# A 16-head cross-attention's last unit turned ahead of an awaited transfer, its second batch in a bank of its own, and each layer's last expert rounded two units sooner

## The reference

```python
# per layer in (L0, L2, L3): context 2 x 2048 x 128, mask 2 x 2048
q = (layernorm(x) @ Wq)            # 16 heads of 128
k, v = ctx @ Wk, ctx @ Wv          # 8 heads of 128, each shared by 2 query heads
p = softmax(mask(q @ k.T / sqrt(128)))
x = x + (p @ v) @ Wo
...
# the last block, L3_ffn: a mixture of 8 experts whose weights are first rounded
# to 8-bit floats, with one power-of-two scale for each block of 32
w13q = mxfp8_qdq(w13);  w2q = mxfp8_qdq(w2)
```

## Time and profile before

| | us |
|---|---|
| median of 3 runs | 1428.22 |
| lowest and highest run | 1422.49, 1431.65 |
| the profiled execution | 1422.41 |
| its span, first to last instruction | 1420.7 |
| TensorE matmul / VectorE / ScalarE / GpSimd busy | 87% / 77% / 65% / 21% |

### The profile page before, as it was taken

The page is one execution under the profiler, slowest core; times in us unless marked ns, Lnnn a source line. Parts: engine busy times, 40 slices in busy tenths (PEclk is TensorE's granted clock), DMA queues, the critical chain, the costliest instruction groups (busy, mean ns, idle before and its releaser), DMA issues. The chain is left out here.

```text
span 1420.7 us, 25856 instructions
## 1 busy us (share of the span) xinstructions
PE 1231.3 (87%) x10032; PEld 848.7 (60%) x10036; DVE 1100.1 (77%) x2026; ACT 919.6 (65%) x1285; POOL 296.0 (21%) x231
## 2 busy tenths in 40 slices
PE   4999999648887998875989999987898899999887
PEld 1677777434334555554756767664586567767654
DVE  5787786396888999927588898857598888889563
ACT  3877777454666777833167777756595767677664
POOL 0000000100251111000005264350263062552400
PEclk9999999979999999987999999999899999999999
DMA  6899989102006999996069999860573799889700
GB/s 249 151 174 187 191 162 159 60 0 97 1 1 118 191 195 187 200 191 144 20 123 182 195 184 184 154 157 17 170 205 118 131 166 177 169 171 169 142 11 8
DMA packets 548298, 195.77 MB, mean 138 GB/s; under 512 B 534880, under 2 KB 535264, under 8 KB 546912
## 3 DMA queue, kind: packets, MB, share of 16 engines
q1 hardware_dynamic: 548192, 194.35, 68.4%
HBM read 59.83 MB, written 0.26 MB: 42 GB/s over the span
## 5 line engine op out<-in xcount | busy, mean ns | idle before, releaser
L687 DVE SCALAR_TENSOR_TENSOR arena<-L_xattn_sm,L_xattn_rr,arena 128x1024 f16<-128x1024 f32 x192 | 278.8, 1493 | 12.1 <-ACT arena L578 12.1
L441 PE MATMUL ps<-ctxT,L_xattn_qk 128*128 128x512 f16 x1152 | 266.3, 381 | 1.7 <-DVE L_xattn_qk L654 1.4
L563 ACT ACTIVATE L_xattn_sm<-L_xattn_sm,L_xattn_mx 128x2048 f32<-128x2048 f32 x96 | 192.3, 2003 | 81.2 <-DVE L_xattn_mx L669 80.2
L578 ACT ACTIVATE arena<-L_xattn_sm,L_xattn_rr 128x1024 f16<-128x1024 f32 x192 | 210.0, 1141 | 5.2
L453 PE MATMUL ps<-arena,ctx 128*128 128x128 f16 x2976 | 187.4, 223 | 16.9 <-DMA arena<-arena 16.7
L453 PEld LDWEIGHTS ps<-arena,ctx 128*128 128x128 f16 x2976 | 175.5, 100 | 32.9 <-DMA arena<-arena 21.6
L441 PEld LDWEIGHTS ps<-ctxT,L_xattn_qk 128*128 128x128 f16 x1152 | 111.5, 99 | 128.1 <-issue 3.7
L669 DVE CUSTOM_DVE_ANT_0 L_xattn_sm<-ps,L_xattn_bias 128x1024 f32<-128x1024 f32 x96 | 117.2, 1221 | 69.9 <-issue 69.6
L669 DVE CUSTOM_DVE_ANT_0 L_xattn_sm<-ps,L_xattn_bias,L_xattn_mx 128x1024 f32<-128x1024 f32 x96 | 123.2, 1284 | 0.8 <-DVE L_xattn_mx L669 0.5
L463 PEld LDWEIGHTS ps<-arena,ctx 128*128 128x128 f16 x1488 | 90.8, 98 | 17.1 <-DMA arena<-arena 0.2
L179 PE MATMUL ps<-ctxT,identh 128*128 128x512 f16 x346 | 91.6, 400 | 7.7 <-PEq L353 3.0
(11 more groups left out here) (539 smaller groups left out, 2109.0 us busy)
## 6 DMA issues: line engine op xcount, KB each, us to landing
L_ffn_ring<-in_L_ffn_experts SPq DMA_DIRECT2D x34, 384.0 KB, 3.6
arena<-in_L_xattn_w SPq DMA_DIRECT2D x36, 320.0 KB, 3.9
arena<-in_L_ffn_experts SPq DMA_DIRECT2D x8, 768.0 KB, 7.8
arena<-in_L_xattn_w SPq DMA_DIRECT2D x6, 640.0 KB, 14.0
arena<-arena SPq DMA_TRANSPOSE x193, 4.5
arena<-in_L_ffn_codes SPq DMA_DIRECT2D x1, 3072.0 KB, 10.9
arena<-in_L_ffn_scales SPq DMA_DIRECT2D x8, 384.0 KB, 22.7
arena<-in_L_attn_w SPq DMA_DIRECT2D x1, 2163.0 KB, 8.7
```

The source lines that it names most:

```text
L441: last = nc.tensor.matmul(ps[:, at, :], qk[:, h // 2, qp, h % 2, b * P:(b + 1) * P], k.ctxT[:, cp, b, at * 512:(at + 1) * 512], start=(a = ...
L563: nc.scalar.activation(sm[:, u % 2, :], sm[:, u % 2, :], ACT.Exp, bias=mx[:, u % 2, 1:2], scale=-1.0, accum_out=rs[:, u % 2:u % 2 + 1]).th ...
L578: nc.scalar.mul(pp[:, u % 2, 0, at], sm[:, u % 2, at], rr[:, u % 2:u % 2 + 1]).then_inc(s.p_high, 1)
L687: nc.vector.scalar_tensor_tensor(pp[:, u % 2, 1, at], sm[:, u % 2, at], rr[:, u % 2:u % 2 + 1], pp[:, u % 2, 0, at], ALU.mult, ALU.subtrac ...
```

## The change

- On TensorE in the last iteration, `turn_last(0)` moves ahead of mix_high(30) and `turn_last(1)` ahead of mix_low(30). In the last body mix_last(0) comes ahead of tail_out(head 14).
- Unit 31 is multiplied into bank 6 (`PREP`) in place of the second half of `O[1]`, so that batch 0 of head 15 can be copied out while batch 1 is still being made. Copy, Wv, copy and Wo of head 15 run once for each batch at half width (`mixed_last`, `values_last`, `values_copy_last`, `out_last`), batch 0's among the matmuls of unit 31.
- ScalarE's copies of the turned high part move ahead of `values_copy` of head 14.
- The bodies in which experts' exponents are made go from 0, 8, 16, 24 to 0, 8, 16, 22, and those of the rounds from 3, 11, 19, 27 to 3, 11, 19, 25. This concerns L2 and L3 alone.

```diff
+    EXPONENTS_AT, ROUNDS_AT = (0, 8, 16, 22), (3, 11, 19, 25)
...
@@ mix_last
-                                last = nc.tensor.matmul(O[1][:, P:2 * P], k.ctx[:, cp, KT + kt, :], pt[:, 1, part, kt, :],
+                                last = nc.tensor.matmul(PREP[:, P:2 * P], k.ctx[:, cp, KT + kt, :], pt[:, 1, part, kt, :],
...
+                def values_last(b):
+                    pe.wait_ge(s.oT_ready, XH + b)
+                    at = slice(b * P, (b + 1) * P)
+                    nc.tensor.matmul(TAIL[1 - b][:, at], wv[1], oT[:, at], start=True, stop=True).then_inc(s.oh_psum, 1)
+
+                def out_last(b):
+                    pe.wait_ge(s.oh_ready, XH + b)
+                    nc.tensor.matmul(OUT[:, b * D:(b + 1) * D], oh[:, b * P:(b + 1) * P], wo[1][:, 1, :], start=False,
+                                     stop=True, skip_group_check=True).then_inc(s.out_done, 1)
@@ TensorE's body
                         if final and u == UNITS - 1:
+                            mix_last(0)
                             tail_out(*mixed)
                             break
+                        if final and u == UNITS - 2:
+                            turn_last(0)
                         mix_high(i, u)
...
                         if final and u == UNITS - 2:
-                            turn_last(0)
+                            turn_last(1)
                         mix_low(i, u)
...
                 iterations(pe, body)
-                turn_last(1)
-                mix_last(0)
+                values_last(0)
                 mix_last(1)
-                tail_values(LASTI, BODY - 1, False)
-                tail_out(LASTI, BODY - 1)
+                out_last(0)
+                values_last(1)
+                out_last(1)
@@ ScalarE
+                def mixed_last(b):
+                    at = slice(b * P, (b + 1) * P)
+                    act.wait_ge(s.mixed_lo, XH * B - 1 + b)
+                    nc.scalar.mul(oT[:, at], (O[1], PREP)[b][:, at], 1.0 / XPUP).then_inc(s.oT_ready, 1)
+
+                def values_copy_last(b):
+                    at = slice(b * P, (b + 1) * P)
+                    act.wait_ge(s.oh_psum, XH + b)
+                    act.wait_ge(s.out_done, XH - 1)
+                    nc.scalar.copy(oh[:, at], TAIL[1 - b][:, at]).then_inc(s.oh_ready, 1)
...
+                        if final and u == UNITS - 2:
+                            last_copy(0, 0)
+                            last_copy(0, 1)
                         if head:
                             values_copy(*head, first and u == 2)
...
                 iterations(act, body)
-                last_copy(0, 0)
-                last_copy(0, 1)
                 last_copy(1, 1)
-                mixed_copy(LASTI, BODY - 1)
-                values_copy(LASTI, BODY - 1, False)
+                mixed_last(0)
+                values_copy_last(0)
+                mixed_last(1)
+                values_copy_last(1)
@@ VectorE
-                        if experts is not None and u == 0:
-                            expert_exponents(k, dve, weigh, experts + i)
-                        if experts is not None and u == 3:
-                            expert_rounds(k, dve, weigh, experts + i)
+                        if experts is not None and UNITS * i + u in EXPONENTS_AT:
+                            expert_exponents(k, dve, weigh, experts + EXPONENTS_AT.index(UNITS * i + u))
+                        if experts is not None and UNITS * i + u in ROUNDS_AT:
+                            expert_rounds(k, dve, weigh, experts + ROUNDS_AT.index(UNITS * i + u))
...
-                dve.wait_ge(s.out_done, XH)
+                dve.wait_ge(s.out_done, XH + 1)
```

More of the change, by code:

```diff
@@ L588, in values_copy, with last_copy @@
                     nc.scalar.copy(oh[:], TAIL[h % 2]).then_inc(s.oh_ready, 1)
+                def last_copy(part, half):
+                    act.wait_ge(s.last_psum, 2 * part + half + 1)
+                    act.wait_ge((s.mixed_hi, s.mixed_lo)[part], XH * B - 2)
+                    nc.scalar.copy(pt[:, 1, part, half * KT // 2:(half + 1) * KT // 2, :], TURNED[2 * part + half])\
+                        .then_inc((s.last_hi, s.last_lo1)[part], 1)
+                def mixed_last(b):
[7 more added lines that the diff above has]
+                    nc.scalar.copy(oh[:, at], TAIL[1 - b][:, at]).then_inc(s.oh_ready, 1)
                 def body(i, first, final):
```

## The result

The changed kernel takes 1437.41 us, the median of twelve runs (1432.78 to 1440.93); the kernel before, measured beside it, 1429.30 (twelve runs, 1421.04 to 1431.65). The ratio is 1.0065, with an interval of 1.0048 to 1.0081: 9.3 us slower on 1428, with 6.9 and 11.6 as its ends. That is more than the 5.9 forecast and above the band of +4 to +7.5 that was given 50%; the time lies inside the range of 1426 to 1440.

The account below looks back on a forecast made before the run. VectorE was taken to set when unit 31 is ready in L3, with L2 its twin. L0 -1.5, L2 +3.55, L3 +3.55 and clock +0.3 gave +5.9, or 1434.0 us; 8-in-10 range 1426 to 1440.

Parts of the forecast that it names:

- L0: At L0's end, the reorder alone shortens mix_high(30) to the last addition from 11.53 to 10.0 us: -1.5 us.
- The contention: In L2 and L3, GpSimd's earlier pass lengthens p_low(29) and p_low(30), so invert(31) starts 3.5 us later per layer.
- about one addition: On VectorE in L2 and L3, each half of p_low(29) and p_low(30) is delayed by one GpSimd addition beyond its own 1.24 us.
- The exponents' move: In L2 and L3, making the last expert's exponents after unit 24's p_low costs 0, bounds 0 and +0.5 us.
- The reorder on top: In L2 and L3, turn_last(0) makes TensorE wait for unit 31's high part; mix_high(30) starts at 1323.95, x 10.0 us later.
- The clock: TensorE's idle time before turn_last(0) in L2 and L3 lowers its clock, mostly within the wait: +0.3 us in all.
- half clock in both tails: Rival: TensorE runs at half clock in L2's and L3's tails, +3.4 in place of 0.3, +9.0 us in all; chance 10%.
- GpSimd's hold: At the block's end in L2 and L3, GpSimd's drain no longer holds the block, saving 0.2 us per layer.

Follow-up runs that it names:

- the kernel with the busy matmuls: The changed kernel with 11 unused matmuls on TensorE ahead of turn_last(0) in L2 and L3: 1432.68 us, ratio 1.0036 to the kernel before.

## Why the prediction was right, and where its size was off

**L0: right.** Forecast -1.5, 10.0 from mix_high(30) to the addition; the trace has 10.00. The turn lies inside the wait for the transfer, as forecast, though mix_high(30) starts 0.26 us later behind invert(31) than it did (3.65 for 3.39). That distance goes from 3.2 to 3.6 over the traces, and is 3.6 in the one with the expert alone moved, so the turn need not be the cause. The gain of the whole layer's block was 1.3.

**The contention: right in kind, place and size.** The forecast was made from the rounds' end. Measured from there (1305.58 in L3): p_low(28) at +2.6 taking 3.13 (forecast +2.8, 3.10), the additions at +8.5 (+8.4), p_low(29) at +9.8 taking 4.33 (+8.7, 5.5), p_low(30) at +16.9 taking 4.16 (+17.0, 4.15). Invert(31) comes 28.44 us after scores(28) in L3, 3.3 more than before; forecast 3.5. In L2 it is 29.98, 4.9 more. The experiment without the pass shows the cause, that with the expert alone moved the size (+3.3 in each). Part of the agreement is luck: scores(30), which the forecast left at 12.01 us behind scores(28), came at 13.1 and 13.8, and p_low(29) met less of the pass for it.

The turns that p_low and the additions take are again as the Trainium skill has them (SBUF — State Buffer, section Who interferes with whom): two SBUF inputs on VectorE and a reading instruction of GpSimd exclude each other. The runs agree, 5.57 us with the additions and 2.48 without them. They agree on GpSimd's side too: in the changed kernel's L3 the addition that starts while a half of p_low is running takes 2.79 us, and one that starts while none is takes 1.82. With the latter figure the prediction's "about one addition" for each half, 1.55 us on top of its own 1.24, is about right; the mean of 2.28 us that the earlier trace rows gives contains GpSimd's own waits.

**The exponents' move: mis-sized.** I took 0, with bounds 0 and +0.5. It is 1.3 to 1.4 by itself. The step that failed is the list of what follows the moved instruction: I counted VectorE's 1.9 us and TensorE's wait for a later high part, but not that SP has a load of weights to issue ahead of this unit's transfer, that the two come closer together (1.18 us apart in the changed kernel's L3, for 2.80), and that the transfer then takes 6.8 us to land in place of 4.3. Together with the rounds' move it isn't added in full: in L3 it bought back about as much contention (4.33 in place of 5.57), in L2 hardly any (5.44). So invert(31) came 0.2 us sooner than forecast in L3 and 1.4 later in L2. That this is the exponents' move is argued, from scores(30) coming late; measured against the rounds' move alone it is worth -1.3 and +0.3.

**The reorder on top: right in kind.** Forecast: invert(31) to mix_high(30) 3.2 us, then 10.0, released by ScalarE after an idle time of some 3 us. The idle time was 3.00 and 2.81, released by L592. At full clock the distances were 3.21 and 9.99 (the kernel with the busy matmuls). What the forecast did not see is how much better the other order is in a late tail: 11.5 in place of 13.2, 1.7 us per layer.

**The clock: the term that was too small.** I added 0.3 in all, bounds 0 and 3.4, on the argument that the dip would fall mostly into the wait. It fell behind it. Invert(31) to the last addition took 15.34 and 14.83 in place of 13.2: 3.8 us, over the upper bound, which had allowed 1.7 for a tail. L2's cost 2.1, of which some 1.7 lie in mix_high(30) and 0.4 ahead of it, in the turn. Its rival "half clock in both tails", given 10%, is what happened; it named +9.0. That this is so close to the measured 9.3 is luck in part, since its other terms are the forecast's. The row that should have weighed more is the earlier trace rows's first: 2.2 us of idle time, and 0.57 of the clock over the next 4 us, in one of two places. The idle time foreseen was longer than that, in both layers. The Trainium skill (TensorE: Matmul & The Clock Gate, section The HAM clock gate) says that idleness brings the array back to half its clock; the two windows at 0.50 and 0.65 agree, and the busy matmuls, with 1.00, show that it is this idle time.

**GpSimd's hold: right.** Its drain is over 14 us before the block's end in L3, and the hold, forecast at 0.2 for each layer and in fact 0.3 and 0.2, is gone.

**The sum.** Forecast -1.5 + 3.55 + 3.55 + 0.3 = 5.9. In the same terms the traces have -1.5 (L0), 4.9 + 0.3 in L2 and 3.3 + 0.2 in L3 for invert(31) and the turn ahead at full clock, 3.8 for the clock and -0.5 for the hold: +10.5, or +10.6 with the hundredths. The measurement has 9.3, between 6.9 and 11.6. Of the 4.7 us between the sums 3.5 are the clock and 1.2 is invert(31), 1.4 later than forecast in L2 and 0.2 sooner in L3.

**What stays open.** Why the granted clock differs from one trace to the next in the last block, whose code doesn't change, and why it fell in L2's tail and not in L3's behind idle times of 1.5 to 1.9 us. The reorder alone gains 2.3 to 3.4 by the ratios, where its tails show 1.0 at best; the rest isn't explained. Of the versions run it is the only one with a ratio below 1 whose interval excludes 1, and in the repeat the interval reaches 1. One would keep it because it is no slower.

## What to carry to other kernels

An instruction that waits for a late input should not be put ahead of work that is ready sooner: the same reorder gave 1.5 us where the input was early, and cost 6.3 where another edit had made it late, so two edits that each cost little have to be priced together. Moving work of a side engine means asking which instructions of the main chain it will meet and how many fit under it: a pass that met one unit on the path and one beside it now met three on the path. When a chain is delayed, follow it into the queue that issues its transfers, and see what that queue issues just ahead; and where an idle time of 2 to 3 us appears ahead of a TensorE chain, price the units behind it at either clock, since it fell here behind all four such waits ahead of the turn (2.18 to 3.00 us).

## What the runs showed of the hardware

- The same transposing transfer, of unit 27's high part in L3, took 4.3 us to land 2.80 us behind a load's issue, 4.5 us at 2.32 behind it, 6.3 at 1.34 and 6.8 at 1.18, and 5.9 without the load ahead of it.
- With the turn ahead of mix_high(30) in L2 and L3, mix_high(30) was slow behind idle times of 3.00 and 2.81 us (3.25 and 3.62 us) and of 2.34 and 2.18 (2.45 and 2.42), and in L2 behind 1.53, 1.71 and 1.87 (3.37, 3.36 and 3.17). It took 1.95 behind 1.25 in L2 and behind 0.52, 0.95, 1.58 and 1.89 in L3. With matmuls put into the idle time it took 1.95 in each of four tails.
- VectorE's p_low and GpSimd's additions lengthen each other: half a p_low goes from 1.28 us to 2.83, an addition from 1.82 to 2.79.
- GpSimd's drain behind the pass took 3997 and 4862 ns in the changed kernel's L2 and L3, where it was 3016 in the kernel before; it lay beside the path there.
